# A graph layer with linear attention and a mixture of experts on one core: queries and keys computed once and kept, the attention context taken from one count table's products, and a ninth count table

## What the reference computes

```python
xn = _layernorm(x)
# graph convolution: degree-normed sum of the source rows over the edges
h = xn @ W
out = segment_sum(h[src_f] * norm[:, None], dst_f) + conv_bias      # then one norm over all, prelu
# linear attention, 4 heads of 32, with 4 memory columns in front of keys and values
q, k, v = split(rmsnorm(xn, g_pre) @ w_qkv, 3)
q = softmax(q over the 32 features of a head) * 32 ** -0.5
k = softmax(k over all nodes)
context = einsum('bhdn,bhen->bhde', k, v)
out = rmsnorm(einsum('bhde,bhdn->bhen', context, q) @ w_out + b_out, g_out) + xn
x = x + gnn + attention
x = x + experts(_layernorm(x))                                      # top 2 of 8, GELU
```

## Time and profile before

| what | before |
|---|---|
| median of three runs | 1373.55 us |
| lowest, highest | 1370.42, 1374.15 us |
| the profiled execution's own time (its span) | 1377.2 us, 0.27% over the median |
| PE busy | 1245.3 us, 90% of the span |
| POOL busy | 854.3 us, 62% |
| DVE busy | 962.4 us, 70% |
| ACT busy | 539.3 us, 39% |
| gathers in the edge stage | 484, issued from 142.8 to 766.8 us |
| last sum of a gathered group | starts at 786.06 us |

### The profile page before, as it was taken

The page is one execution under the profiler, slowest core; times in us unless marked ns, Lnnn a source line. Parts: engine busy times, 40 slices in busy tenths (PEclk is TensorE's granted clock), DMA queues, the critical chain, the costliest instruction groups (busy, mean ns, idle before and its releaser), DMA issues. The chain is left out here.

```text
span 1377.2 us, 30864 instructions
## 1 busy us (share of the span) xinstructions
PE 1245.3 (90%) x8354; PEld 1106.3 (80%) x8355; DVE 962.4 (70%) x2966; ACT 539.3 (39%) x1443; POOL 854.3 (62%) x836
## 2 busy tenths in 40 slices
PE   4997688999899999999898797985799999999998
PEld 4984687887788888887787686873699999999997
DVE  8998787887888777778693288998444444444444
ACT  7707301222333333333311101446455555555553
POOL 1294677777777777777777202431376666666665
PEclk9999899999999999999999898995799999999999
DMA  7005333335666666789898400449244444444443
GB/s 245 0 0 183 111 106 103 107 105 172 194 194 199 198 191 202 207 246 277 260 288 261 144 1 16 138 155 318 64 77 66 68 71 69 72 69 70 71 69 42
DMA packets 138148, 186.89 MB, mean 136 GB/s; under 512 B 21438, under 2 KB 116468, under 8 KB 137916
## 3 DMA queue, kind: packets, MB, share of 16 engines
q0 software_dynamic: 43440, 90.29, 28.7%
q1 hardware_dynamic: 94604, 95.40, 21.8%
HBM read 153.16 MB, written 33.41 MB: 135 GB/s over the span
## 5 line engine op out<-in xcount | busy, mean ns | idle before, releaser
L740 POOL DMA_INDIRECT RG<-table,srci x484 | 477.3, 986 | 153.0 <-issue 149.4
L757 PEld LDWEIGHTS ps<-S_t,RG 128*128 128x128 f32 x1936 | 259.2, 196 | 39.0 <-DMA RG<-table,srci 28.6
L757 PE MATMUL ps<-S_t,RG 128*128 128x96 f32 x1936 | 266.4, 278 | 21.6 <-DMA RG<-table,srci 21.1
L780 PE MATMUL ps<-zrow,R 128*128 128x256 f32 (+1 forms) x784 | 221.1, 389 | 15.2 <-DMA zrow<-table 8.7
L2010 POOL DMA_INDIRECT out<-R,S_t x105 | 166.3, 1584 | 99.5 <-DVE R L1980 55.8
L1893 PE MATMUL ps<-R,RG 128*128 128x128 f32 x1680 | 207.3, 277 | 0.0
L1893 PEld LDWEIGHTS ps<-R,RG 128*128 128x128 f32 x1680 | 198.3, 194 | 0.4 <-issue 0.4
L1903 PE MATMUL ps<-R 128*128 x840 | 198.5, 379 | 0.0
L1014 DVE TENSOR_TENSOR R<-R,ps 128x245 f32 (+4 forms) x300 | 142.1, 474 | 73.7 <-PE ps L768 52.5
L1926 ACT ACTIVATE R<-ps,RG 128x128 f32<-128x128 f32 x420 | 120.0, 368 | 175.8 <-PE ps L1893 175.8
L1976 DVE TENSOR_TENSOR R<-ps,R 128x256 f32<-128x256 f32 x105 | 44.6, 425 | 200.8 <-PE ps L1903 200.8
(11 more groups left out here) (360 smaller groups left out, 1989.9 us busy)
## 6 DMA issues: line engine op xcount, KB each, us to landing
zrow<-table SPq DMA_DIRECT2D x384, 128.0 KB
RG<-table,srci POOLq DMA_INDIRECT x484, 3.3
ntable<-R SPq DMA_DIRECT2D x12, 516.0 KB
table<-RG SPq DMA_DIRECT2D x12, 512.0 KB, 2.9
out<-R SPq DMA_DIRECT2D x12, 512.0 KB, 3.2
R<-in_x SPq DMA_DIRECT2D x6, 896.0 KB, 11.7
R<-in_w SPq DMA_DIRECT2D x8, 514.0 KB, 6.4
slot<-in_x SPq DMA_DIRECT2D x32, 128.0 KB
```

The source lines that it names most:

```text
L740: nc.gpsimd.indirect_dma_start(out=grows[:, s, :], out_offset=None, in_=table, in_offset=bass.IndirectOffsetOnAxis(ap=srci[:, ND + q, c:c ...
L757: last = nc.tensor.matmul(window(q % 2)[:, h, :], grows[:, s, h * P:(h + 1) * P], S_t[:, q % 2, c, :], start=c == 0, stop=c == GC - 1)
L780: nc.tensor.matmul(psD[:, 0:D], adj[b % 2][0:n, j, :], zrow[0:n, i % ZR, :], start=j == 0, stop=j == T - 1).then_inc(z_used, 1)
```

## The change

Four things are done at once, all in the edge stage.

- A ninth table: `DBLK` gets a block of four more groups (75 to 79), so 117 groups are gathered, with 468 transfers. The new block, which is the smallest, is counted and multiplied first (`ORDER`). `BUILT` and `USED` deal the tables anew.
- The 49 tiles of queries and keys are computed together and once (`queries_keys`, 256 columns), in the first 28 groups; ACT copies them over the tile of `zT` that they came from (`stash`). The maximum of the keys, the keys less the maximum and the query's softmax read them from there.
- The context is no longer made of values. `product` of the second table in order (`GP = 1`) is followed by a second product with the same z tile: the tile's exponentiated keys, weighted (`keys_exp`, `weight_column`, `keys_weighted`), times its 256 columns and one more, a weight. The sum over all tiles is turned and multiplied with the values' weights once, after the last tile.
- The stretches of the attention move: keys and queries 0 to 28, the context 31 to 49, the output rows 53 to 102 (before 37 to 88), the residual 105 to 115 of 117 (before 91 to 119 of 121). The output product has two PSUM banks.

```diff
 OHB = NC // OHC
 OHR = 4
 assert OHB % OHR == 0
-DBLK = ((0, 27), (27, 38), (38, 46), (46, 53), (53, 59), (59, 65), (65, 70), (70, 75))
+DBLK = ((0, 27), (27, 38), (38, 46), (46, 53), (53, 59), (59, 65), (65, 70), (70, 75), (75, 79))
 ND = DBLK[-1][1]
 NDB = len(DBLK)
-DWB = (5, 5, 6, 7, 8, 8, 8, 9)
+DWB = (5, 5, 6, 7, 8, 8, 8, 9, 9)
 DW = max(DWB)
 DLIM = P - DW
 MD = ND * GC
+ORDER = (NDB - 1,) + tuple(range(NDB - 1))
+CHUNK = [g * GC + c for b in ORDER for g in range(*DBLK[b]) for c in range(GC)]
+ENDS = [sum(DBLK[b][1] - DBLK[b][0] for b in ORDER[:p + 1]) * GC for p in range(NDB)]
+GP = 1
 RUNS = [(min(g0 for (g0, _), k in zip(DBLK, DWB) if k == d), max(g1 for (_, g1), k in zip(DBLK, DWB) if k == d), d)
         for d in sorted(set(DWB))]
 assert all((d - 1) * -(-WIN // d) < WIN for d in DWB) and list(DWB) == sorted(DWB) and T * DW <= 512
...
-        A0, A1 = 0, 12
-        C0, C1 = 14, 34
-        B0, B1 = 37, 88
-        D0, D1 = 91, GQ - 2
-        BUILT = (0, 33, 47, 61, 74, 86, 95, 104, 112)
-        USED = (33, 47, 61, 74, 86, 95, 104, 112, GQ - 2)
+        A0, A1 = 0, 28
+        B0, B1 = 53, 102
+        D0, D1 = 105, GQ - 2
+        BUILT = (0, 5, 31, 49, 58, 68, 77, 87, 96, 106)
+        USED = BUILT[1:] + (GQ - 2,)
+        G1 = USED[GP + 1]
+        assert A1 + 2 <= USED[GP] and G1 + 3 <= B0
 
         def share(q, lo, hi, n):
 
...
+        def ahead(q, r):
+
+            q, r = (q, r + 1) if r < 3 else (q + 1, 0)
+            return [j for b, j in quarter(products(q), r) if b == GP]
 
         phase = []
         with nc.Block(no_gpsimd_drain=True) as block:
...
                 def product(b, j):
...
                     if j == 0:
-                        pe.wait_ge(cnt_ok, DBLK[b][1] * GC)
+                        pe.wait_ge(cnt_ok, ENDS[b])
                         if b > 0:
                             pe.wait_ge(blk_ok, b)
                     n = P if j < T - 1 else TAIL
-                    nc.tensor.matmul(psD[:, 0:D], adj[b % 2][0:n, j, :], zrow[0:n, i % ZR, :], start=j == 0,
-                                     stop=j == T - 1).then_inc(z_used, 1)
+                    last = nc.tensor.matmul(psD[:, 0:D], adj[b % 2][0:n, j, :], zrow[0:n, i % ZR, 0:D], start=j == 0,
+                                            stop=j == T - 1)
+                    if b == GP:
+                        pe.wait_ge(rc_ok, j + 1)
+                        pe.wait_ge(ex_ok, j + 1)
+                        last = nc.tensor.matmul(psC[:, 0:D + 1], esl[0:n, j % 2, :], zrow[0:n, i % ZR, :], start=j == 0,
+                                                stop=j == T - 1)
+                    last.then_inc(z_used, 1)
...
-                def keys(t):
+                def queries_keys(t):
                     if t >= 2:
-                        pe.wait_ge(k_max, t - 1)
+                        pe.wait_ge(st_ok, t - 1)
                     for k in range(KC):
-                        last = nc.tensor.matmul(psA[t % 2][:, 0:P], zT[:, k, t * P:(t + 1) * P], wqkv[:, k, P:2 * P],
+                        last = nc.tensor.matmul(psA[t % 2], zT[:, k, t * P:(t + 1) * P], wqkv[:, k, 0:2 * P],
                                                 start=k == 0, stop=k == KC - 1)
                     last.then_inc(k_ps, 1)
-                def keys_values(t):
-                    if t >= 2:
-                        pe.wait_ge(ks_ok, t - 1)
...
...
-                        nc.tensor.matmul(psC[:, 0:P + 1], emT[:, :], mvT[:, :], start=True, stop=False,
-                                         skip_group_check=True)
-                    for s in quarter(share(q, C0, C1, T + 1), r):
-                        if s < T:
-                            keys_values(s)
-                        if s >= 1:
-                            context(s - 1)
-                    if q == C1 + 1 and r == 2:
+                    if q == G1 and r == 2:
                         pe.wait_ge(mid_dve, 4)
+                        for k in range(KC):
+                            last = nc.tensor.transpose(psA[0][:, k * P:(k + 1) * P], sums[:, k * P:(k + 1) * P], ident[:, :])
+                        last.then_inc(mid_pe, 1)
+                    if q == G1 + 1 and r == 0:
+                        pe.wait_ge(mid_dve, 5)
+                        for k in range(KC):
+                            nc.tensor.matmul(psA[1][:, 0:P], turned_sums[:, k * P:(k + 1) * P], wqkv[:, k, 2 * P:3 * P],
+                                             start=k == 0, stop=False)
+                        nc.tensor.matmul(psA[1][:, 0:P], emT, mvT, start=False, stop=True).then_inc(mid_pe, 1)
+                    if q == G1 + 1 and r == 2:
+                        pe.wait_ge(mid_dve, 6)
                         nc.tensor.transpose(psT, cn, ident[:, :]).then_inc(mid_pe, 1)
-                    if q == C1 + 2 and r == 2:
-                        pe.wait_ge(mid_dve, 5)
-                        nc.tensor.matmul(psO, cnT, wout[:, :], start=True, stop=True).then_inc(mid_pe, 1)
-                        pe.wait_ge(mid_dve, 6)
+                    if q == G1 + 2 and r == 0:
+                        pe.wait_ge(mid_dve, 7)
+                        nc.tensor.matmul(psO[0], cnT, wout[:, :], start=True, stop=True).then_inc(mid_pe, 1)
+                    if q == B0 and r == 0:
+                        pe.wait_ge(mid_dve, 8)
                     for s in quarter(share(q, B0, B1, T + 3), r):
-                        if s < T:
-                            queries(s)
                         if 0 <= s - 2 < T:
                             flip(s - 2)
...
-                def values(t):
-                    act.wait_ge(ks_ok, t + 1)
-                    if t >= 2:
-                        act.wait_ge(cx_ok, t - 1)
-                    act.activation(vsl[:, t % 2, 0:P], psA[t % 2][:, P:2 * P], ACT.Copy,
-                                   scale=cq[:, t:t + 1]).then_inc(v_ok, 1)
-
-                def keys_exp(t):
-                    act.activation(esl[:, t % 2, :], ksl[:, t % 2, :], ACT.Exp).then_inc(ex_ok, 1)
+                def stash(t):
+                    act.wait_ge(k_ps, t + 1)
+                    act.activation(o_tile(t), halved(psA[t % 2]), ACT.Copy).then_inc(st_ok, 1)
+
+                def keys_exp(j):
+                    act.wait_ge(ks_ok, j + 1)
+                    if j >= 2:
+                        act.wait_ge(z_used, GP * T + j - 1)
+                    act.activation(esl[:, j % 2, :], ksl[:, j % 2, :], ACT.Exp).then_inc(er_ok, 1)
+
+                def weight_column(j):
+
+                    i = GP * T + j
+                    act.wait_ge(z_used, i - ZR + 1)
+                    act.activation(zrow[:, i % ZR, D:D + 1], rcq[:, j:j + 1], ACT.Copy).then_inc(rc_ok, 1)
+
+                def keys_weighted(j):
+                    act.wait_ge(er_ok, j + 1)
+                    act.activation(esl[:, j % 2, :], esl[:, j % 2, :], ACT.Copy, scale=cq[:, j:j + 1]).then_inc(ex_ok, 1)
 
                 def q_power(t):
                     act.wait_ge(q_sub, t + 1)
...
-                        for s in quarter(share(q, C0, C1, T + 1), r):
-                            if s < T:
-                                values(s)
-                                keys_exp(s)
+                        for t in quarter(share(q, A0, A1, T), r):
+                            stash(t)
+                        for j in ahead(q, r):
+                            keys_exp(j)
+                            weight_column(j)
+                            keys_weighted(j)
                         for s in quarter(share(q, B0, B1, T + 3), r):
                             if 0 <= s - 2 < T:
                                 qt_out(s - 2)
...
                 def keys_max(t):
-                    v.wait_ge(k_ps, t + 1)
+                    v.wait_ge(st_ok, t + 1)
                     scale = cq[:, t:t + 1]
                     if t == 0:
-                        nc.vector.tensor_scalar(cn, psA[0][:, 0:P], scale, None, ALU.mult).then_inc(k_max, 1)
+                        nc.vector.tensor_scalar(cn, key_of(t), scale, None, ALU.mult).then_inc(k_max, 1)
                         return
                     v.wait_ge(k_max, t)
                     n = P if t < T - 1 else TAIL
-                    nc.vector.scalar_tensor_tensor(cn[0:n, :], psA[t % 2][0:n, 0:P], scale[0:n, :], cn[0:n, :], ALU.mult,
+                    nc.vector.scalar_tensor_tensor(cn[0:n, :], key_of(t)[0:n, :], scale[0:n, :], cn[0:n, :], ALU.mult,
                                                    ALU.max).then_inc(k_max, 1)
 
-                def keys_less_max(t):
-                    v.wait_ge(kv_ps, t + 1)
-                    if t >= 2:
-                        v.wait_ge(ex_ok, t - 1)
-                    nc.vector.scalar_tensor_tensor(ksl[:, t % 2, :], psA[t % 2][:, 0:P], cq[:, t:t + 1], mrow, ALU.mult,
+                def query_of(t):
+                    return o_tile(t)[:, 0, :]
+
+                def key_of(t):
+                    return o_tile(t)[:, 1, :]
+
```

(47 more changed lines are left out.)

112 lines of the change are left out of this document (52 added, 60 removed).

## The result

The changed kernel took 1406.07 us, the median of four runs (1402.29 to 1407.54), with 1373.85 for the kernel before, measured beside it. The ratio is 1.0229, with an interval of 1.0206 to 1.0253: slower by some 32 us. The forecast was 1372.6 with a range of 1352 to 1388, so the time lies outside it; "slower" had a chance of 0.37.

The account below looks back on a forecast made before the run. POOL's gathers were taken to bound the edge stage. Start 697, nine residual cycles of 80 and 8 for the end gave 785 against before's 786.4; with 0.4 added, −1.0 on 1373.55, so 1372.6 us, range 1352 to 1388.

Parts of the forecast that it names:

- the start of the residual's stretch: Sum of group 105: POOL's pace up to there unchanged, so 695, plus 2 us for stretched gathers, 697.
- 8 for the end: After the last group with x tiles: two more groups' aggregate halves and sums, taken as 8 us, stage ending at 785.
- the waits for the exponentials: Groups 31 to 48: context products wait on PE for weighted exponentials, 21 us together, 1.2 a group; cost nothing overall.
- The lag: Groups 31 to 48: PE needs 5.6 us a group against POOL's 5.1, so 9 us of lag build up.
- The room: Gather ring of 16 slots holds 20 us; before's lag takes 10 of them, so PE's new lag just fits.
- The repayment: After the context groups PE catches up; groups 53 to 102 need 4.9 to 5.1 us, under POOL's 5.17.
- second rival: Context groups: waits fill the gather ring, POOL stops for 17 us not given back before group 105; 1386, chance 0.11.
- the residual's cycle of 8.9 us: Groups 105 to 114: x tiles' round trip through a ring of three takes 8.9 us a group, nine cycles, 80 us.
- first rival: Last groups: x tiles are hidden, stage ends 27 us earlier, 1346; halfway cases 1355; chance 0.20 with these.
- third rival: Last groups: x tiles land behind z-tile bursts at 5.8 us instead of 3.9, 17 us more, 1390; chance 0.09.
- The new neighbours of the gathers: Edge stage: keys' and query's DVE instructions now read two SBUF inputs, stretching 40 gathers by 0.05, 2 us on POOL.
- fourth rival: Edge stage: gathers stretched as by one-hots, 14 us instead of 2, 1385, at half of that 1378; chance 0.08.

Follow-up runs that it names:

- The run with two quarters' lead and the original ring: The change with the weighted exponentials made two quarters ahead instead of one, in four buffers, keeping its ring of three for the x tiles: 1382.64 us, 1.0061 of before.
- eight tables: The change without the ninth table, with x tiles in a ring of eight and exponentials two quarters ahead: 1363.23 us, 0.9905 of before.
- the deep ring: The change with the residual's x tiles in a ring of eight in a free count table, residual from group 106: 1380.71 us, 1.0051 of before.
- the late residual in the kernel before: The kernel before with the residual dealt over its last ten groups (109 to 119) instead of 28: 1401.91 us, 1.0216 of before.
- eight tables (and both edits): The change without the ninth table, with x tiles in a ring of eight and keys less maximum ahead of the count sums: 1370.82 us, 0.9963 of before.
- the best version found: The change with x tiles in a ring of eight and weighted exponentials two quarters ahead, in four buffers: 1360.26 us, again 1360.17, 0.9882 of before.

## Why the prediction was wrong

The sum had three terms: the start of the residual's stretch at 697, its length of 80, and 8 for the end, 785 in all. Measured: 727.6, 83.4, and 4.4 to the end of the last sum at 815.4. Two terms hold within 4 us. The step that failed is the first term: "It just fits, and PE catches up afterwards. I cost it at nothing." The 30.6 us that are missing there are the result. The run with two quarters' lead and the original ring starts this stretch at 704.5: 23.1 of the 30.6 us are the waits for the exponentials, which I had priced at 21 us on PE and at nothing on the kernel, and 7.5 are left.

Three things were wrong in that step.

- The lag. I let 9 us build up in groups 31 to 48 and nothing before or behind. The price of the waits about held: PE stood 16.8 us for the exponentials, and from group 33 to 47 it took 5.85 us a group with them and 4.66 without, so 1.2 a group, as forecast. But the lateness shows 6.6 already between groups 27 and 33, of which 1.1 is left without these waits, and 15 from 47 to 60, which doesn't hang on them. I had not priced the latter. The set-up of the output product falls there (PE waits 1.4 and 1.5 us ahead of L852 and L860, at 428 and 436 us), and so does a table that is multiplied in nine groups; that the tables' dealing has the larger part is argued from the 10 us that eight tables take off, and not shown by a run of its own. The cause of the 5.6 us up to group 27, where 2.4 were forecast for the whole stage, stays open; with nine tables every version of the change has 5 to 6 of them.
- The room. I took 10 us as free in the ring, from a lag of 10 us between a group's last gather and its sum that I had worked out from the mean spacing of the gathers. Before's own trace has 13.9 at the 105th sum (its gather starts at 680.58) and 11.5 at group 27. In the trace after, the lag of a sum behind the end of its last gather was 12.7 us at group 24 and 18 to 27 from group 33 to 60, when POOL stops. Some 7 were left. And the room is asked for twice: without the waits the lag, from the last gather's start, falls to 9.3 us at group 47, and the next 13 groups bring it to 21.5 all the same.
- The repayment. PE's 4.9 to 5.1 a group in groups 53 to 102 was nearly right from group 60 on, where it is busy 5.04 a group, and so was POOL's 5.2. But a difference of 0.1 in 45 groups repays 5 us at most. From group 60 to group 102 the change took (716.4 − 497.6) / 42 = 5.21 a group, before (678.7 − 461.3) / 42 = 5.17. What PE is late at group 60 stays. A stretch from 488 us on shows it with nothing left (PE 19.76 of 20.00):

```profile
488.00:508.00 20.00, 19.76 (x129) 17.40 (x128) 17.54 (x65) 8.03 (x26) 15.12 (x17) 1.00 0.79 232
```

This is the second rival in kind (the gather ring fills, POOL stops, nothing gives it back), at about twice its price: it had 17 us, the waits alone cost 23, and it had no other source of lateness. Its chance of 0.11 was too low: the forecast's margin, 9 of 10 us, was smaller than the error of each of the two numbers.

What was right: the residual's cycle of 8.9 us for five tiles (measured 8.8 between bursts), with its cause; the deep ring and the late residual in the kernel before confirm it from both sides. The x tiles were not hidden (first rival), and did not land later than before (third rival). The new neighbours of the gathers cost about what was forecast, partly by luck: 26 gathers start inside the three kinds of instructions (with one of them the last that DVE had begun), where I had 40, and are longer than 0.946 by 2.5 us together, against 2 (fourth rival down); each costs 0.10, where I had 0.05.

A deeper point was missed. Counted from the trace, the time in which PE or its weight load runs, from 150 us to the end of the stage, is 587 us before and 584 after. But the granted clock is at its lower level in 22 us of the one and 49 of the other; counted at the clock granted it is 576 and 560. So keeping the queries and keys saved PE 16 us more than the ninth table and the second product of each z tile added. POOL's 468 gathers of 1.25 are 585. Over the whole stage PE thus has 4% less to do than POOL, and such a margin is easily read as room. It isn't spread evenly: from group 47 to 60 PE is busy 5.4 us a group, over POOL's pace, and from 60 to 102 5.04 of 5.21, which leaves nothing to catch up with. With eight tables (and both edits) it is 4.65 of 4.95 there. That goes with the ninth table, worth 20 us to POOL, being worth hardly anything to the kernel, and with the best version found, 1360.2 us, 14 to 15 us less than before measured beside it, getting there by taking waits away.

## What to carry to other kernels

When an engine that sets the pace is relieved, work out the work of the next engine stretch by stretch before counting the gain; where the two have nearly the same pace, a wait counts in full once the buffer between them is full, and a lag is not caught up later. When work is dealt over fewer groups, look at each ring that it goes through: a ring of three that was no wait at one or two tiles a group set the pace at five. A forecast that rests on a fit by one part in ten should be priced as if it doesn't fit.

## What the runs showed of the hardware

A gather can be stretched by far more than the 0.10 and 0.35 us of the earlier trace rows where two DVE instructions with both inputs in SBUF follow each other, here the maximum of the keys and a group's one-hots:

```profile
248.07 0.35 DVE L1038 SCALAR_TENSOR_TENSOR slotb<-R,cq,slotb 128x128 f32<-128x128 f32 x1
...
248.16 1.55 POOL L755 DMA_INDIRECT RG<-table,srci  x1 [0.30 <-issue]
248.34 0.55 DVE L983 TENSOR_TENSOR S_t<-dstrel,iwin 128x384 f32<-128x384 f32 x1
```

This gather took 0.60 longer than 0.946. Another, at 177.81 us, starts as far into a maximum, with the one-hots as close behind, and took 1.52. Two that start 0.14 and 0.15 us into a maximum with no one-hots beside them took 1.02 (at 235.48 and 282.53). So the 0.60 can't be put down to the maximum alone. One that starts 0.03 us into it, with the one-hots behind, took 0.95 (at 183.44); why stayed open.

The other half of the rule that the prediction's fourth rival quotes, that a DVE instruction with at most one input in SBUF does not contend, is not exact here: 42 gathers start inside the one-hots of a count (L1012, L1013, one tensor from SBUF and a number for each partition) with no instruction of two such tensors beside them, and took 0.96 in the mean and 1.05 at most.

The granted clock of TensorE falls in parts of the residual's stretch of the change, and less with the deep ring. In a stretch of 10 us from 757 to 767 its mean, the seventh number column from the left, behind POOL's, is 0.73, so it was partly at the lower of its two levels (1.2 GHz); the second row is from the run with the deep ring:

```profile
757.00:767.00 10.00, 7.53 (x29) 6.05 (x29) 4.88 (x13) 2.78 (x5) 4.93 (x5) 0.73 0.72 223
```

```profile
755.00:765.00 10.00, 7.56 (x44) 6.17 (x44) 7.58 (x20) 3.86 (x8) 7.35 (x8) 1.00 1.08 347
```

PE is busy for the same share in both, with 29 instructions in the one and 44 in the other. The deep ring doesn't rule it out: with two quarters' lead on top the stretch from 710 to 720 us has 0.83. What the lower clock cost isn't separated by a run; the residual's steps had nearly the length that the estimate of the transfers gives them, 8.8 for 8.9.
